# Reordering a fused recurrent block and ternary FFN on one core: gates before the w1/w3 products, conv before quantisation, the recurrence between g steps

## The reference

```
xn  = layernorm(x)
# recurrent branch (L = 256 channels, 4 taps)
y    = gelu(xn @ w_y + b_y);  xb = xn @ w_x + b_x
conv = conv_b + sum_k conv_w[k] * xb shifted by 3-k tokens
gate_x = sigmoid(conv @ w_ig + b_ig);  gate_a = sigmoid(conv @ w_ag + b_ag)
log_a = -8 * gate_a * softplus(a_param);  a = exp(log_a);  mult = sqrt(1 - a*a)
(first token: a = 0, mult = 1);  h_t = a_t * h_(t-1) + gate_x * conv * mult
attn = (h * y) @ w_out + b_out
# FFN branch (682 hidden), weights made ternary: clip(round(w/s), -1, 1) * s, s = mean |w|
ffn = (silu(xn @ w1q.T) * (xn @ w3q.T)) @ w2q.T
out = x + attn + ffn
```

## Time and profile before

| | |
|---|---|
| median of 3 runs | 89.52 us (88.8 to 89.9) |
| profiled execution, first to last instruction | 87.7 us |
| busy: DVE, PE, POOL, ACT | 73.9, 72.9, 54.4, 51.8 us |
| DMA | 5.75 MB, nearly all in the first 17.5 us |

### The profile page before, as it was taken

The page is one execution under the profiler, slowest core; times in us unless marked ns, Lnnn a source line. Parts: engine busy times, 40 slices in busy tenths (PEclk is TensorE's granted clock), DMA queues, the critical chain, the costliest instruction groups (busy, mean ns, idle before and its releaser), DMA issues.

```text
span 87.7 us, 1098 instructions
## 1 busy us (share of the span) xinstructions
PE 72.9 (83%) x376; PEld 61.9 (71%) x376; DVE 73.9 (84%) x107; ACT 51.8 (59%) x80; POOL 54.4 (62%) x47
## 2 busy tenths in 40 slices
PE   5991999999999999649799999999999830199950
PEld 5980798988878877418476888879999820199840
DVE  0189987599999999999999665999999929999970
ACT  4643799696999994505394987978966020202200
POOL 7205500050965199998099997699999999490000
PEclk9999759999999999999999999999999999555999
DMA  1999999300000000000000000000000000000085
GB/s 17 303 288 332 342 358 366 110 7 0 0 4 0 0 0 0 0 0 0 0 4 0 0 7 0 0 0 0 0 0 0 0 0 0 0 7 0 0 271 207
DMA packets 5141, 5.75 MB, mean 66 GB/s; under 512 B 444, under 2 KB 4624, under 8 KB 5136
## 3 DMA queue, kind: packets, MB, share of 16 engines
q1 hardware_dynamic: 4992, 5.68, 19.4%
q10 hardware_dynamic: 144, 0.01, 0.2%
HBM read 4.64 MB, written 1.05 MB: 65 GB/s over the span
## 4 chain that ended last, share of the span: by engine, by line
DVE 38%; PE 26%; POOL 17%; issue 10%; DMA 4%; ACT 2%; DVEq 1%; POOLq 0%
DVE conv L524 17%; POOL x_sb L236 13%; PE slot L663 8%; PE slot L680 7%; DVE tx L574 5%; PE slot L761 5%; DVE w_raw L551 5%; DMA x_sb<-x 4%; PE slot L722 3%; DVE tx L576 3%; POOL g_lo L246 2%; PE slot L652 2%; DVE xn_y L472 2%; DVE stats L447 2%; POOL tx L269 1%
## 5 line engine op out<-in xcount | busy, mean ns | idle before, releaser
L246 POOL TENSOR_TENSOR g_lo<-w_raw,g_hi 128x512 fp32r<-128x512 f32 x10 | 17.1, 1727 | 3.7 <-ACT g_hi L357 3.0
L680 PE MATMUL slot<-xt_hi,w_q 128*128 128x512 f32 x40 | 16.0, 401 | 0.8 <-DVE w_raw L551 0.7
L680 PE MATMUL slot<-xt_lo,w_q 128*128 128x512 f32 x40 | 15.7, 394 | 0.0
L524 DVE SCALAR_TENSOR_TENSOR conv<-xb,par,conv 128x512 f32<-128x512 f32 x12 | 15.3, 1327 | 0.0
L236 POOL TENSOR_TENSOR x_sb<-x_sb,b_out_bc 128x256 f32<-128x256 f32 x8 | 11.8, 1509 | 0.0
L221 POOL TENSOR_TENSOR w_lo<-w_raw,w_hi 128x512 fp32r<-128x512 f32 x5 | 6.9, 1382 | 7.0 <-ACT w_hi L282 7.0
L722 PE MATMUL slot<-w_hi,conv_hi 128*128 128x256 f32 x16 | 5.6, 364 | 5.9 <-ACT conv_hi L395 5.8
L680 PEld LDWEIGHTS slot<-xt_hi,w_q 128*128 128x128 f32 x40 | 7.5, 188 | 3.7 <-DVE w_raw L551 2.1
L228 POOL TENSOR_SCALAR conv<-xb,par 128x512 f32<-128x512 f32 x4 | 3.9, 982 | 9.9 <-ACT xb L330 9.9
L357 ACT ACTIVATE g_hi<-w_raw 128x512 fp32r<-128x512 f32 x8 | 5.0, 628 | 8.2 <-DVE w_raw L551 8.2
L710 PE MATMUL slot<-w_q,g_hi 128*128 128x256 f32 x40 | 9.5, 281 | 0.0
(11 more groups left out here) (113 smaller groups left out, 188.6 us busy)
## 6 DMA issues: line engine op xcount, KB each, us to landing
w_raw<-w13t SPq DMA_DIRECT2D x2, 682.0 KB, 8.1
w_raw<-dense SPq DMA_DIRECT2D x5, 256.0 KB, 7.7
out<-x_sb SPq DMA_DIRECT2D x3, 256.0 KB, 2.2
w_raw<-w2t SPq DMA_DIRECT2D x1, 640.0 KB
x_sb<-x SPq DMA_DIRECT2D x2, 256.0 KB, 3.3
x_sb<-x SPq DMA_DIRECT2D x1, 512.0 KB, 5.7
out<-x_sb SPq DMA_DIRECT2D x2, 128.0 KB, 2.1
b_out_bc<-b_out SPq DMA_DIRECT2D x1, 128.0 KB, 7.1
```

The costliest lines, as they stand in the source:

```text
L246: nc.gpsimd.tensor_tensor(g_lo[:, j, s], g[:, n % RING], g_hi[:, j, s].bitcast(f32), ALU.subtract).then_inc(g_lo_set, 1)
L524: nc.vector.scalar_tensor_tensor(out=conv[:, s, c], in0=xb[:, s, c, k:k + SEQ], scalar=par[:, CONV_W + KC * k + c:CONV_W + KC * k + c + 1] ...
L680: mm = nc.tensor.matmul(slot[H_SLOT[s][j]][:, o], w13_q[:, c, col:col + P], v[:, s, c], start=(c == 0 and v is xt_hi), stop=(c == KC - 1 a ...
```

## The change

The same arithmetic, in another order, with these differences:

- DMA: w_ig and w_ag are loaded ahead of w1/w3. b_out is loaded as one row, split into hi and lo, and the two parts are written by DMA into rows 42 and 43 of w2's last block; the rows of `gt` that meet them are set to 1, so that down adds b_out. `residual` is gone.
- Gates: all four gate products stand ahead of hidden(0); the sums for the thresholds are matmuls in the middle of gate products.
- DVE: all conv taps stand ahead of the w1/w3 quantisation; the recurrence of each sequence (`recurrence`, `gated_output`) stands between g steps; the product with mult is whole on DVE.
- POOL: waits for the normalised tiles before its first subtraction; all `lo_of_g`, then all four `lo_of_hy`.
- ScalarE: Ln ahead of the first root; Exp and Sqrt of both sequences in one stretch between silu(4) and silu(5), so there is one more return to Silu.
- TensorE: down(0) stands between hidden(4) and hidden(5), project(0) ahead of down(1).

```diff
+        T_SLOT, X_SLOT, Y_SLOT = (0, 1), (2, 0), (3, 2)
+        GX_SLOT, GA_SLOT = (1, 3), (0, 2)
+        H_SLOT = ((1, 0, 2, 1, 0), (2, 1, 0, 2, 1))
+        O_BANK = ((slot[3][:, 0], slot[3][:, 1]), (slot[0][:, 0], slot[0][:, 1], slot[2][:, 0]))
...
@@ sync
             square(WY)
+            square(WIG)
+            square(WAG)
             w13_dram = w13t.rearrange("(c p) n -> p c n", p=P)
...
-            square(WIG)
-            square(WAG)
             square(WOUT)
-            sp.dma_start(b_out_bc[:, :], b_out.partition_broadcast(P)).then_inc(b_out_loaded, 16)
+            sp.dma_start(b_row[:, :], b_out.rearrange("(o d) -> o d", o=1)).then_inc(b_out_loaded, 16)
+            sp.wait_ge(w2_q_set, 1)
+            sp.wait_ge(b_split_set, 1)
+            for k in range(2):
+                sp.dma_start(w2_q[TAIL + k:TAIL + k + 1, FULL].bitcast(f32), b_split[:, k].bitcast(f32)).then_inc(b_placed, 16)
...
@@ gpsimd
+            def lo_of_hy(s):
+                for c in range(KC):
+                    pool.wait_ge(hy_hi_set, KC * s + c + 1)
+                    nc.gpsimd.tensor_tensor(conv_lo[:, s, c], tx[:, s, c], conv_hi[:, s, c].bitcast(f32), ALU.subtract).then_inc(hy_lo_set, 1)
+            pool.wait_ge(xn_set, TILES)
             square_lo(WX)
             square_lo(WY)
+            square_lo(WIG)
             pool.wait_ge(par_loaded, 16)
             newest_tap(0)
+            square_lo(WAG)
             newest_tap(1)
-            square_lo(WIG)
-            square_lo(WAG)
             lo_of_conv(0)
+            lo_of_conv(1)
             square_lo(WOUT)
+            pool.wait_ge(b_hi_set, 1)
+            nc.gpsimd.tensor_tensor(b_split[:, 1], b_row[:, :], b_split[:, 0].bitcast(f32), ALU.subtract).then_inc(b_split_set, 1)
+            for n in range(2 * FULL):
                 lo_of_g(n)
-            residual(0)
-            residual(1)
             for s in range(SEQS):
...
+                lo_of_hy(s)
...
@@ scalar, order after the first Exp
+            (Ln) root_of(0) square_hi(WX) xt_hi_of(0) square_hi(WY) root_of(1) square_hi(WIG) xb_of(0) xt_hi_of(1)
+            abs_sum w1, square_hi(WAG) xb_of(1) conv_hi_of(0) abs_sum w3, gelu_of(0) conv_hi_of(1) gelu_of(1)
+            gate_x(0) abs_sum w2, gate_a(0) square_hi(WOUT) b_split hi, gate_x(1) gate_a(1)
+            silu_of(0) silu_of(1) g_hi_of(0) silu of the tail, g_hi_of(1) silu_of(2) silu_of(3) g_hi_of(2) silu_of(4)
+            g_hi_of(3) g_hi_of(4) decays(0) decays(1) mult_of(0) mult_of(1) silu_of(5) silu_of(6) g_hi_of(5)
+            hy_hi_of(0, 0) hy_hi_of(0, 1) silu_of(7) g_hi_of(6) silu_of(8) g_hi_of(7) silu_of(9) g_hi_of(8) g_hi_of(9)
+            hy_hi_of(1, 0) hy_hi_of(1, 1)
@@ vector, order after variance(1)
+            xt_lo_of(0) normalise(1) half_b, older_tap(0, 1) xt_lo_of(1) older_tap(0, 2) older_tap(0, 3) first_mult(0)
+            older_tap(1, 1) older_tap(1, 2) threshold_13() older_tap(1, 3) first_mult(1) ternary_13() gated_input(0)
+            threshold_2() ternary_w2() a_rate, g_of(0) g_of(1) gated_input(1) g_t, g_of(2) gt_hi, gt, g_of(3) gt lo, g_of(4)
+            squares(0) squares(1) recurrence(0) g_of(5) gated_output(0, 0) gated_output(0, 1) g_of(6) recurrence(1)
+            g_of(7) gated_output(1, 0) gated_output(1, 1) g_of(8) g_of(9) output(0..4)
...
             def recurrence(s):
-                nc.vector.tensor_tensor(tx[:, s, 0], tx[:, s, 0], xb[:, s, 0, TAPS - 1:], ALU.mult).then_inc(nx_set, 1)
+                dve.wait_ge(mult_set, KC * (s + 1))
+                nc.vector.tensor_tensor(tx[:, s], tx[:, s], xb[:, s, :, TAPS - 1:], ALU.mult).then_inc(nx_set, 1)
...
@@ tensor
+            gate_product(0, WIG, GX_SLOT, gx_psum, sums_of_w13)
+            pe.wait_ge(thr_set, 3)
+            gate_product(0, WAG, GA_SLOT, ga_psum)
+            pe.wait_ge(y_set, KC)
+            gate_product(1, WIG, GX_SLOT, gx_psum, sum_of_w2)
+            pe.wait_ge(y_set, 2 * KC)
+            gate_product(1, WAG, GA_SLOT, ga_psum)
             pe.wait_ge(w13_q_set, 2)
             pe.wait_ge(s2_ready, 3)
             hidden(0)
+            (hidden 1, the tail, 2, 3, 4, each behind its slot's reader)
+            pe.wait_ge(w2_q_set, 1)
+            pe.wait_ge(g_t_set, 1)
+            down(0)
+            (hidden 5 to 9, hidden(n) behind g_set n - 2)
+            project(0)
+            pe.wait_ge(g_set, 9)
             down(1)
             project(1)
```

More of the change, by code:

```diff
@@ L403, in _ @@
             silu_of(1)
-            conv_hi_of(0)
+            g_hi_of(0)
+            act.wait_ge(t_psum, 1)
+            act.wait_ge(w_lo_set, WOUT + 1)
+            nc.scalar.activation(silu_t[HALF:HALF + TAIL], slot[TAIL_SLOT][0:TAIL].rearrange("p s n -> p (s n)"), ACT.Silu,
+                                 scale=scale[0:TAIL, 0:1]).then_inc(silu_t_set, 1)
+            g_hi_of(1)
             silu_of(2)
-            g_hi_of(0)
-            square_hi(WOUT)
-            g_hi_of(1)
             silu_of(3)
@@ L412, in _ @@
             g_hi_of(3)
+            g_hi_of(4)
+            decays(0)
+            decays(1)
+            mult_of(0)
+            mult_of(1)
             silu_of(5)
-            g_hi_of(4)
             silu_of(6)
             g_hi_of(5)
-            conv_hi_of(1)
-            gate_x(0)
+            hy_hi_of(0, 0)
+            hy_hi_of(0, 1)
+            silu_of(7)
             g_hi_of(6)
[L420 to L425, removed]
             silu_of(8)
@@ L428, in _ @@
             silu_of(9)
[L429 to L437, removed]
+            g_hi_of(8)
+            g_hi_of(9)
+            hy_hi_of(1, 0)
+            hy_hi_of(1, 1)
         @block.vector
@@ L489, in _ @@
[L489 to L513, removed]
@@ L590, in output @@
                                         x_sb[:, s, t], ALU.add).then_inc(o_set, 1)
+            for i in range(2):
+                dve.wait_ge(x_loaded[i], 16)
+                statistics(0, range(i * TILES // 2, (i + 1) * TILES // 2))
+            variance(0)
+            normalise(0)
+            dve.wait_ge(x_loaded[2], 16)
+            statistics(1, range(TILES))
+            variance(1)
+            xt_lo_of(0)
+            normalise(1)
+            dve.wait_ge(par_loaded, 16)
+            nc.vector.tensor_scalar(half_b[:, :], par[:, B_IG:B_IG + 2 * KC], 0.5, None, ALU.mult).then_inc(half_b_set, 1)
+            older_tap(0, 1)
+            xt_lo_of(1)
+            older_tap(0, 2)
+            older_tap(0, 3)
+            first_mult(0)
+            older_tap(1, 1)
+            older_tap(1, 2)
+            threshold_13()
+            older_tap(1, 3)
+            first_mult(1)
+            ternary_13()
+            gated_input(0)
+            threshold_2()
+            ternary_w2()
             dve.wait_ge(sp_log, 1)
@@ L782, in _, with gate_product @@
             dense_terms(slot[X_SLOT[1]], WX, [(w_hi, xt_lo[:, 1])], False, True).then_inc(xb_psum, 1)
-            dense_product(slot[Y_SLOT[1]], WY, xt_hi[:, 1], xt_lo[:, 1], y_psum, between=sum_of_w2)
+            dense_terms(slot[Y_SLOT[0]], WY, [(w_hi, xt_lo[:, 0])], False, True).then_inc(y_psum, 1)
+            pe.wait_ge(xb_set, KC)
+            dense_product(slot[Y_SLOT[1]], WY, xt_hi[:, 1], xt_lo[:, 1], y_psum)
+            def gate_product(s, m, slots, done, between=None):
+                pe.wait_ge(w_lo_set, m + 1)
+                dense_product(slot[slots[s]], m, conv_hi[:, s], conv_lo[:, s], done,
+                              (conv_hi_set, KC * s + 1), (conv_lo_set, KC * s + 1), between)
+            gate_product(0, WIG, GX_SLOT, gx_psum, sums_of_w13)
[5 more added lines that the diff above has]
+            gate_product(1, WAG, GA_SLOT, ga_psum)
             pe.wait_ge(w13_q_set, 2)
```

234 lines of the change are left out of this document (104 added, 130 removed).

## The result

The changed kernel takes 96.59 us (median of 4 runs, 96.05 to 97.52) against 89.48 us before (88.8 to 89.9). The ratio is 1.079, 95% interval 1.071 to 1.087: 7.9% slower. The forecast was 96.0, range 91.8 to 99.0.

The account below looks back on a forecast made before the run. It took DVE, blocked in turn by POOL, as the bound; g(9) at 75.45, POOL's subtractions to 80.5, 74 matmuls to 91.1 and 3.1 us more gave span 94.2, plus 1.8 makes 96.0 us, range 91.8 to 99.0.

Parts of the forecast that it names:

- The bound of before: Kernel before: the chain of waits is mostly DVE's, 38% of the span, held up by POOL and ending on the last multiply by y.
- The price list: Times set per operation on each engine, such as 0.118 us a 256-column matmul and 1.26 a POOL subtraction.
- Start: Front of the kernel: root 0.8 us later at 6.5, normalised tiles out at 9.1, xb(0) readable at 14.05.
- the walk: The prediction's step-by-step passage through the engines' queues, from start to tail, ending at a span of 94.2 us.
- Middle: Conv, quantisation and gates: POOL blocks DVE, WAG(0) waits 1.7 us, hidden(0) starts at 40.1 on the w2 threshold.
- Table switch and recurrence: Between silu(4) and silu(5): 9.4 us of ScalarE, mult(0) at 61.1, then DVE's scans and g steps to g(9) at 75.45.
- Tail: End of the kernel: four POOL subtractions to 80.5, then 74 matmuls, 8.7 us plus 1.8 for half clock, last at 91.1.
- A: Rival: slower but less, as the middle's DVE/POOL blocks fall in gaps; 92.3 us, chance 0.20.
- B: Rival: not slower, as DVE and POOL never meet at the port; 88.0 us, chance 0.08 including a way toward A.
- point of no change: In the tail: the time of hy_lo(0,1), about 74 us, at which the changed kernel would equal the one before.
- C: Rival: TensorE at half clock for the whole tail, 7.0 us in place of 1.8; 101.2 us, chance 0.12 with its neighbours.
- D: Rival: b_out's rows land late, so down(0) isn't hidden; 96.0 to 98 us, chance 0.05 within the forecast's.

Follow-up runs that it names:

- e5: Changed kernel with POOL's subtractions for w_lo of WAG and WOUT and for conv_lo cut to 8 columns, the rest zero; 93.03 us, ratio 1.049 to the kernel before.
- e7: Changed kernel with project(0)'s lo terms behind down(1), sequence 1's hy_lo on DVE, idle products, w2 threshold ahead of gated_input(0), Ln just before Gelu; 87.21 us, ratio 0.983.
- e1: Changed kernel with TensorE's down(1) ahead of project(0), nothing else; 92.9 us, ratio 1.040 to the kernel before.
- e2: Changed kernel with POOL's two hy_lo subtractions of sequence 0 moved between g_lo(6) and g_lo(7); 92.55 us, ratio 1.036 to the kernel before.
- e4: Changed kernel with nine added unread products of ones on TensorE between project(0)'s hi and lo terms; 95.17 us, ratio 1.062 to the kernel before.
- e8: Kernel before with only b_out through w2's spare rows and no residual adds, POOL's small b_out subtraction behind lo_of_conv(1); 85.98 us, ratio 0.965.
- e6: Kernel before with only b_out through w2's spare rows and no residual adds, POOL's small b_out subtraction ahead of g_lo(0); 88.97 us, ratio 0.998.

## Why the prediction was right

**The bound of before, and the port.** The price list held but for two entries (below). DVE's work on operands in SBUF takes the sum of both beside POOL's, in the changed kernel (10.32 against 5.09 us in e5: five POOL operations, 1.05 each) as in the earlier trace rows. That holds for the first pass over w1/w3 too, which has one tensor operand (3.89 against 1.79). The Trainium skill (SBUF — State Buffer, SBUF: two separate sides) calls the shared port pair an exclusive lock, held for a whole instruction; the rows of e5 and of the changed kernel agree with it.

**Start.** Ln got a load of its own behind Exp, and the root came at 6.40 (6.5 predicted):

```profile
3.59 1.28 ACT L308 ACT_TABLE_LOAD   x1
4.88 0.20 ACT L308 ACTIVATE sp_e<-sp_e 128x2 f32<-128x2 f32 x1
5.11 1.28 ACT L282 ACT_TABLE_LOAD   x1
6.40 0.30 ACT L282 ACTIVATE ln<-mv,eps 128x4 f32<-128x4 f32 x1
```

So Exp and Ln did not share a load, though the Trainium skill (ScalarE: Activation LUTs, Table sets) knows one set that holds both; the first load was not of that set. Ln had a load of its own in before (14.24) and in e7 (23.54) too. Nor did these loads show the drain of 1.38 us that the same page of the Trainium skill adds to each switch: each of these loads is followed by its activation within 0.02 us, and starts within 0.03 of the end of the one before. The four normalised tiles took 1.38 us, as predicted. xb(0) was 1.1 late in this profile, 0.3 in e1's. Most of it is the clock of the stretch, which I had taken from before and which differs between profiles: the walk had the products of xt_lo at full clock, and here the clock is at 0.50 until 14.5 us, in e1 until 13.5.

**Middle.** The order of waits was as walked: WAG(0) waits for the threshold (0.68 us idle where 1.7 was predicted, since the product before it ended 1.1 us later than walked, 28.05 for 26.95 in e1, 0.58 of it in its own wait for conv_lo), the w2 sum in the middle of WIG(1) (1.00 for 1.4), hidden(0) for the w2 threshold (1.05 for 1.6). hidden(0) is within 0.2 us of the prediction in e1's profile. Two prices were off and fell beside other work: the a_rate step took 0.36 us (43.51 to 43.87) where 0.8 was set, the small b_out subtraction 1.70 where nothing was set.

**Table switch and recurrence.** 9.4 us of ScalarE before silu(5) were predicted, from 55.41 to 64.84 they are 9.43. From mult(0) to g(9) 14.35 were predicted and 14.3 came.

**Tail.** This was the largest step. g(9) came 4.6 us earlier than the last product of before (5.7 predicted), and behind it stood 15 us to the last matmul of the chain, where before 3.1 stood (81.17 to 84.28). The terms came as summed: the four subtractions took 4.95 us (5.1 predicted), from there to the last of the 74 matmuls it was 10.9 (10.6), and from that to the end of the span 3.1 (3.1). e1 and e2 show from either side that it is the two orders together: with one changed, 3.7 and 4.0 us are gone. They do not decide the sign alone: e1 and e2 are still 4.0 and 3.6% slower than the kernel before, and only the four repairs of e7 bring it under. e4 shows the clock's share, 1.4 in time and 2.1 in its profile (predicted 1.8).

**Rivals.** A needed blocks that fall in gaps; e5 shows that they did not. B's point of no change was hy_lo(0,1) at 74; it came at 81.7. B without any block had hidden(0) at 35.1, 5.0 us ahead of the forecast; e5, with nearly all blocks of the middle gone, has it at 36.4, where TensorE takes over as the bound, and gains 2.7 to 3.6 us in time, so B overrated it. C did not come: 20 matmuls ran at half clock, the rest of the 74 at full. D did not come: the two row DMAs were issued at 43.62 and landed 1.7 us after their issue (no row of before had shown such a transfer), down(0) waited for g_lo(3) and (4) alone, and gt's four matmuls went at 57.86 with no wait.

What the walk had wrong is small and of both signs, and the clock of the front and of the tail, taken from one profile of before, differs by some tenths of a us from one profile to the next; that the sum is within 0.6 us is in part luck.

## What to carry to other kernels

Work taken off the path early is given back if the queue behind it is in the wrong order: before moving a stage, list for each engine what stands between its last input and the end, here four subtractions and 74 matmuls. Of two engines that share a port, the price of an operation on SBUF operands is its whole length on the other's queue, and where it stands decides whether anyone pays. Where a matrix engine must wait shortly before its last long stretch, filling that wait with idle products can be worth more than it costs (1.4 us in e4). Try each part of a change alone: here one part by itself (e8) took 3.5% off, and the whole added 7.9%.

## What the runs showed of the hardware that was not expected

The port isn't always taken in turn. In e6 DVE's product came 0.04 us behind POOL's first g_lo and waited for three of them, so that it took 4.28 us; in e8, with the same queues in another phase, it took 1.11, 0.5 of it waiting. By the section of the Trainium skill named above, whoever starts first blocks the other for the whole instruction; here it was three instructions, and no run shows what decides who is next. A kernel that is one small operation away from such a phase can lose 2 us by it.

Tiny operations pay the full block as well. In the changed kernel the same product of 4 numbers a partition took 0.16 us in the first sequence and, beside POOL's subtraction for w_lo, 1.20 in the second:

```profile
7.22 0.16 DVE L465 SCALAR_TENSOR_TENSOR ln<-ln 128x4 f32<-128x4 f32 x1
...
12.67 1.20 DVE L465 SCALAR_TENSOR_TENSOR ln<-ln 128x4 f32<-128x4 f32 x1
```

A POOL subtraction of 256 numbers on one partition took 1.70 us beside DVE's work and 0.73 in e5 and e8.
